# Layer 1, first two aggregation runs: normed rows split in half precision before four half transposes, and the linear products moved into the following run

## The reference

```python
    def _L1_gnn_ref(x, adj, W1, b1, W2, b2, W3, b3, g1, be1, g2, be2, g3, be3):
        ...
        dinv = jnp.sum(adj, axis=-1) ** (-0.5)
        A = adj * dinv[:, None] * dinv[None, :]
        h1 = x @ W1 + b1
        n1 = _layernorm(jax.nn.relu(A @ h1) + h1, g1, be1)
        h2 = n1 @ W2 + b2
        n2 = _layernorm(jax.nn.relu(A @ h2) + n1, g2, be2)
        h3 = n2 @ W3 + b3
        n3 = _layernorm(jax.nn.relu(A @ h3) + n2, g3, be3)
        return n3
```

## Time and profile before

| what | value |
|---|---|
| median of 3 runs | 2527.01 us (2522.1, 2527.01, 2527.02) |
| the profiled execution: its time, and its span in the trace | 2532.7 us, 2530.9 us |
| PE busy / DVE / ACT / POOL over the span | 81% / 62% / 43% / 18% |
| mean granted TensorE clock | 0.912 |
| `P1`, first two aggregations' tails | from 485.15 us to 875.07 us of the span |

### The profile page before, as it was taken

How to read it: one execution, slowest core, us unless ns; L and a number is a source line. 1 busy time by engine, 2 the same in 40 slices (tenths; PEclk the granted TensorE clock), 3 DMA queues, 4 the chain that set the end, 5 groups by cost and what they waited for, 6 DMA issues and landing times. The chain is left out here.

```text
span 2530.9 us, 47194 instructions
## 1 busy us (share of the span) xinstructions
PE 2061.4 (81%) x17042; PEld 1374.8 (54%) x17042; DVE 1560.9 (62%) x3094; ACT 1081.5 (43%) x2337; POOL 458.3 (18%) x437
## 2 busy tenths in 40 slices
PE   7899185999999999648885699569877999996597
PEld 3788153688888888535553587456653222221243
DVE  6665654644445566654437788544466999996543
ACT  6454264511112244326654677236555242323353
POOL 0000463100000022124441134145420000001100
PEclk9899597999999999869997899789988999998598
DMA  4998359164554689635525466412232332321001
GB/s 141 314 354 294 109 138 253 53 247 184 236 222 197 252 315 333 230 129 184 184 68 160 118 177 157 169 56 72 66 112 75 105 110 81 89 81 43 6 0 44
DMA packets 232448, 389.44 MB, mean 154 GB/s; under 512 B 19952, under 2 KB 185457, under 8 KB 215730
## 3 DMA queue, kind: packets, MB, share of 16 engines
q1 hardware_dynamic: 208982, 338.35, 39.7%
q0 software_dynamic: 13760, 39.68, 5.9%
q10 hardware_dynamic: 9504, 8.65, 1.1%
HBM read 306.74 MB, written 79.89 MB: 153 GB/s over the span
## 5 line engine op out<-in xcount | busy, mean ns | idle before, releaser
L1003 PE MATMUL ps<-R,BIG 128*128 128x256 f16 (+1 forms) x1936 | 534.7, 276 | 23.1 <-DVE BIG L1501 13.4
L1004 PE MATMUL ps<-R,BIG 128*128 128x256 f16 x1936 | 531.1, 274 | 0.0
L1005 PE MATMUL ps<-R,BIG 128*128 128x256 f16 (+1 forms) x1936 | 530.9, 274 | 0.0
L2494 PE MATMUL ps<-BIG 128*64 128x452 f32 x1056 | 235.3, 567 | 30.3 <-DVE BIG L2625 26.1
L1995 DVE TENSOR_TENSOR X<-X 128x512 f16<-128x512 f32 (+1 forms) x152 | 85.3, 562 | 270.6 <-ACT X L1974 254.8
L1003 PEld LDWEIGHTS ps<-R,BIG 128*128 128x128 f16 x1936 | 188.7, 97 | 59.1 <-DVE BIG L1501 13.7
L261 PE MATMUL ps<-X,BIG 128*128 128x128 f16 x904 | 189.5, 227 | 29.2 <-issue 16.1
L1004 PEld LDWEIGHTS ps<-R,BIG 128*128 128x128 f16 x1936 | 191.1, 99 | 23.9
L1005 PEld LDWEIGHTS ps<-R,BIG 128*128 128x128 f16 x1936 | 189.2, 98 | 26.9
L2625 DVE SCALAR_TENSOR_TENSOR BIG<-BIG 128x904 f32<-128x904 f32 x176 | 192.4, 1156 | 4.8 <-DVE BIG L2620 4.0
L263 PE MATMUL ps<-X,BIG 128*128 128x128 f16 x904 | 190.1, 228 | 4.6 <-issue 4.3
(11 more groups left out here) (378 smaller groups left out, 4602.4 us busy)
## 6 DMA issues: line engine op xcount, KB each, us to landing
BIG<-adj_split SPq DMA_DIRECT2D x66, 1408.0 KB, 12.9
BIG<-in_adjT SPq DMA_DIRECT2D x42, 1408.0 KB, 11.1
adj_split<-BIG SPq DMA_DIRECT2D x22, 1408.0 KB
BIG<-in_adj SPq DMA_DIRECT2D x22, 1408.0 KB, 6.3
BIG<-in_adjT SPq DMA_DIRECT2D x66, 452.0 KB, 3.3
XX<-in_f SPq DMA_DIRECT2D x64, 256.0 KB, 13.4
experts_split<-XX SPq DMA_DIRECT2D x64, 256.0 KB
BIG<-experts_split SPq DMA_DIRECT2D x16, 1024.0 KB, 12.6
```

What stands on the lines that cost most here:

```text
L1003: pe.matmul(out[:, 0:n], pr[:, 0, k, :], h[:, k, 0:n], start=start, stop=False)
L1004: pe.matmul(out[:, 0:D], pr[:, 0, k, :], l[:, k, 0:D], start=False, stop=False)
L1005: return pe.matmul(out[:, 0:n], pr[:, 1, k, :], h[:, k, 0:n], start=False, stop=stop)
L2494: pe.matmul(ps[rs, 2 * (h // 2) + c, 0:CW], self.G[:, u, h * HF:(h + 1) * HF], self.PT[:, u, h, cs], start=start, stop=stop)
```

## The change

The normed tile is split before it is turned. ACT gets a new step `high(m)`, which copies `nrow` as half precision into `row[:, m % 3, 0:D]`; DVE's subtraction now takes its operands from SBUF, writes the low part into `row[:, m % 3, D:2D]`, and stands before `count`; PE turns the row with four half transposes into one bank, at step 16; ACT's `turned(m)` copies all 512 half columns at once to `xt` (a new semaphore `sq`). `linear(m)` runs at step 2 of the following run m + 2, except for the last tile of an aggregation, where it stays in run m + 1, at step 20.

```diff
                 def turn(m):
-                    s.wait(pe, "ny", m + 1)
-                    s.wait(pe, "xl", m - 1)
-                    for f in range(FT):
-                        mm = pe.transpose(ps[:, 2 + m % 2, f * P:(f + 1) * P], nrow[:, m % KT, f * P:(f + 1) * P], ident[:, :])
+                    s.wait(pe, "xl", m + 1)
+                    s.wait(pe, "sq", m - 1)
+                    for q in range(4):
+                        mm = pe.transpose(ps[:, 2 + m % 2, 0:D].bitcast(F16)[:, q * P:(q + 1) * P],
+                                          row[:, m % 3, q * P:(q + 1) * P], ident16[:, :])
                     mm.then_inc(s["t"], 1)
 
                 def linear(m):
-                    s.wait(pe, "xl", m + 1)
+                    s.wait(pe, "sq", m + 1)
...
                         m = n - 1
-                        if 0 <= m < 2 * KT and k == 14:
+                        if 0 <= m < 2 * KT and k == 16:
                             turn(m)
-                        if 0 <= m < 2 * KT and k == 19:
+                        if 0 <= m < 2 * KT and m % KT == KT - 1 and k == 20:
                             linear(m)
+                        if 0 <= m - 1 < 2 * KT and m % KT and k == 2:
+                            linear(m - 1)
...
+                def high(m):
+                    s.wait(act, "ny", m + 1)
+                    s.wait(act, "t", m - 2)
+                    act.activation(row[:, m % 3, 0:D], nrow[:, m % KT, :], ACT.Copy).then_inc(s["xh"], 1)
+
                 def turned(m):
                     s.wait(act, "t", m + 1)
                     s.wait(act, "mm", m - 3)
-                    act.activation(xt[:, m % 4, 0:2, :], ps[:, 2 + m % 2, 0:D].rearrange("p (f c) -> p f c", f=FT), ACT.Copy)\
-                       .then_inc(s["xh"], 1)
+                    act.activation(xt[:, m % 4, :, :].rearrange("p q c -> p (q c)"), ps[:, 2 + m % 2, 0:D].bitcast(F16), ACT.Copy)\
+                       .then_inc(s["sq"], 1)
...
                     root_act(act, m % 4, 1, s)
+                    high(m)
                     turned(m)
...
                     norm(m, q).then_inc(s["ny"], 1)
+                    s.wait(v, "ny", m + 1)
+                    s.wait(v, "xh", m + 1)
+                    v.tensor_tensor(row[:, m % 3, D:2 * D], nrow[:, t, :], row[:, m % 3, 0:D], ALU.subtract).then_inc(s["xl"], 1)
                     if m % 3 == 1:
                         count(m // 3)
-                    s.wait(v, "xh", m + 1)
-                    v.tensor_tensor(xt[:, m % 4, 2:4, :], ps[:, 2 + m % 2, 0:D].rearrange("p (f c) -> p f c", f=FT),
-                                    xt[:, m % 4, 0:2, :], ALU.subtract).then_inc(s["xl"], 1)
```

More of the change, by code:

```diff
@@ L1188, in __init__ @@
                 self.st = Stage("seq", **{f"d{u}": 16 * T3 // 6 for u in range(6)}, d6=16 * KT, cb=KT,
-                                used=T3, e1=T3, ev=T3, ag=T3 + KT, le=T3 + KT, ny=2 * KT, xh=2 * KT, xl=2 * KT, mm=2 * KT,
+                                used=T3, e1=T3, ev=T3, ag=T3 + KT, le=T3 + KT, ny=2 * KT, xh=2 * KT, xl=2 * KT, sq=2 * KT, mm=2 * KT,
                                 hh=2 * KT, hl=2 * KT, t=T3, **LATER.totals(), dg=14, gm=4, gb=4, **Rows.totals())
```

## The result

| what | before | changed |
|---|---|---|
| median of the runs of this comparison | 2521.64 us (2517.95 to 2527.02, 6 runs) | 2507.03 us (2496.73 to 2512.36, 6 runs) |
| profiled execution: time, span | 2532.7, 2530.9 | 2511.49, 2509.7 |
| raw of tile 0 to raw of tile 44 ("the stage" below) | 389.9 us | 376.6 us |
| PE waits for the low parts before the linear products | 11.7 us, 15 times | none |

The ratio of the two is 0.9935, 95% interval 0.991 to 0.9961: faster by 16.4 us, between 10 and 23. The three runs of before that the prediction had seen were high ones; with three more its median is 2521.64 and not 2527.01. A second comparison, in which the whole kernel runs 2% faster on both sides, gave 2461.49 against 2473.59 us, ratio 0.9953 (0.9937 to 0.997).

A forecast was written before the change was run, and what follows sets the result against it. PE was taken to bound the stage, waiting on low parts behind the count: -14.4 us for 15 tails, +0.7 for two ends, the rest 0, together -13.7, so 2527.0 becomes 2513.3 us; range 2507 to 2520.

The forecast's parts named there:

- What bounds the stage: Both early aggregations of layer 1: TensorE (PE) bounds, losing 0.94 us per count while waiting for DVE's low parts.
- The sum: Stage: 15 tails with a count shed 14.4 us, two aggregation ends cost 0.7, together -13.7 us, 389.9 to 376.2.
- Turn, count, wider copy at nothing: Tails: half transposes take 0.22 us as before; later count and ACT's 27 us more work cost nothing.
- End of an aggregation: Last linear part, twice: one step less cover, loss grows from 0.49 to 0.82 us, cost 0.66 us in all.
- The tail: After raw: root at 2.13 us, norm ends 4.28, ACT copy to 4.73, subtraction to 5.18, turn possible from 5.23.
- The slack of 0.9: Turn at step 16: PE reaches it at 6.12 us, inputs ready from 5.23, so no wait of PE expected.
- that of the first tails (0.3): First tail of an aggregation: turn at 5.05 us against inputs at 4.74, so no wait of PE expected.
- the base: Whole kernel: median 2527.0 us, profiled execution 5.7 us above it, so the changed median should be 2513.3 us.
- Third aggregation and all behind move as they are: Behind the stage: everything starts on its semaphores and should move ahead unchanged, keeping the 13.7 us.
- Rival D: Behind the stage: gain given back as the clock in later slices swings; half might vanish, 2520 us; chance 4%.
- Rival A: Turn: half transposes cost more here; upper bound 9.7 us leaves a gain of 4.0, time 2523; chance 5%.
- B: The 15 tails: another wait, say for an adjacency slot, replaces the removed one; half the gain stays out, 2520; chance 4%.
- C: Turn: PE waits for low parts; a chain 1.2 us longer than laid out eats the gain; slower, chance 2%.

The follow-up runs named there:

- count_behind_only: Kernel before with only DVE's subtraction put ahead of the count, all else as before; stage 376.3 us, ratio 0.995.
- before_again: Kernel before, unedited, traced a second time; 2521.15 us, ratio 1.0008 to the same kernel, stage 389.9 us, third aggregation 182.4 us.
- after_again: Changed kernel, unedited, traced a second time; ratio 0.9953 to the kernel before, stage 376.6 us, third aggregation 183.1 us.
- half_turn_twice: Changed kernel with its four half transposes issued twice (eight); stage 386.4 us.
- count_ahead_again: Changed kernel with the count put back ahead of DVE's subtraction, other parts kept; stage 400.2 us, ratio 1.0059 to the kernel before.
- linear_same_run: Changed kernel with every tile's linear products at step 20 of the run of its own turn; stage 376.9 us, ratio 0.9956.
- tail_longer_2: Changed kernel with ACT's new copy of the rows done three times, tail 0.90 us longer; stage 378.6 us.

## Why the prediction was right or wrong, point by point

- *What bounds the stage* was right: PE, with 0.94 us lost per count. count_behind_only removes that wait alone and has the gain.
- *The sum* was right for its place: -13.7 forecast, -13.3 measured in the stage (376.2 and 376.6 us). Both comparisons hold it: 13.3 us are a ratio of 0.9947, inside 0.991 to 0.9961 and inside 0.9937 to 0.997.
- *Turn, count, wider copy at nothing*: right. The turn takes 0.22 us, the count is done at 8.14, ACT's busy time in the stage went from 75.9 to 103.5 us, the 27 forecast, and nobody waits for it.
- *End of an aggregation*: 0.82 us lost there, as laid out; the last runs are 10.42 and 10.44 us against 10.4, the first 7.45 and 7.43 against 7.45.
- *The tail* was laid out 0.15 us too late. I let the root start when right's record ends; on ACT the next instruction starts about 0.09 us before that (614.31 against 613.93 + 0.47). The slack of 0.9 measures as 0.95, that of the first tails (0.3) as 0.2.
- **The step that failed** is the base: "That execution lies 5.7 us above the median of 2527.0, so the median should be 2513.3". I took three runs for the kernel's level, and set the lower end of the range by the lowest of the three. With three more runs the same kernel had 2521.64, and in the other comparisons 2518.24, 2534.61, 2473.59. The median of 2507.03 lies at the lower edge of the range of 2507 to 2520, and the time by the ratio is 2521.64 x 0.9935 = 2505.2, below it. Of the 6.3 us between forecast and median 5.4 are base. The other 0.9 is 14.6 of difference in medians instead of 13.7. By the ratio the distance to the forecast is 8.1 us, 5.4 of base and 2.7 of gain (16.4 instead of 13.7); the interval of that gain, 10 to 23 us, holds the forecast, so nothing shows the 2.7 to be real.
- *Third aggregation and all behind move as they are* holds on the whole but not in one pair: the third took 6.1 us more, the experts gave back 9. before_again and after_again show scatter of 2 to 3 us in the third, and up to 25 us between comparisons in the experts. *Rival D* named this, with the clock as its cause, and in the third aggregation of the first pair the clock has most of it: 4.2 of the 6 us. Whether the change made it so is open. The 25 us in the experts are not the clock, which was 0.87 and 0.86 there in the two traces of the changed kernel.
- *Rival A* fell (half_turn_twice), *B* did not appear: no wait on a transfer in the stage. *C* is true in kind: the point from which it decides was put at 1.2 us, and it measures 0.95 + 0.33 = 1.3.

## What to carry to other kernels

A long instruction that nobody waits for belongs behind the short one that the bounding engine waits for. Here one swap on DVE holds all of the gain, and the three other parts of the change together add nothing to it (376.3 us without them, 376.6 with them). A wait on a queue delays all that is behind it: 82.8 us of SP waiting looked harmless, and cost 20 to 22 us (183.1 and 185.4 against 163.0) because a store stood behind it, part of it in clock that TensorE lost by standing still. And a difference can be forecast much better than a level: with three runs of a kernel that scatters by 5 us, the range of the absolute time needs the scatter of the level too.

## What the runs showed of the hardware

- A float32 transpose of 128 x 128 costs TensorE 110 ns in a full stream, no more than two half ones of 56 ns.
- In count_ahead_again a wait of TensorE of 2.0 us was followed by 16 matmuls at the 1.2 GHz level, 0.213 us apart instead of 0.11. In the third aggregation the mean granted clock was 0.94 with 12.7 us of idle in 185, and 1.00 with 0.4 in 164.
- In every trace of a kernel with the new subtraction, tiles 14 and 36 (tile 14 of either aggregation) have it start 0.35 us late (in the changed kernel 5.05 us after raw instead of 4.70): DVE idles 0.90 us before it and not 0.55, while ACT's copy before it is on time. It costs 0.15 us per place in linear_same_run and 0.3 in tail_longer_2. The cause was not looked for.
- The same kernel runs 2% faster in some comparisons than in others (before: 2473.59 and 2475.9 us, or 2518.24 to 2534.61), with a granted clock of 0.91 to 0.92 in all. In the changed kernel 25 us of that lie in the experts of layer 1.
